# Reordering the passage from the quantised feed-forward layer into relative-position self-attention

## What is computed

```python
x = _layernorm(x + _L0_xattn_ref(x, ctx, ctx, mask, fside, ...))     # 16 heads of 16, additive bias and mask
x = _layernorm(x + _L0_ffn_ref(x, weight, gamma, beta))
x = _layernorm(x + _L1_attn_ref(x, Wq, bq, Wk, bk, Wv, bv, Wo, bo, rel_k, rel_v))

def _L0_ffn_ref(x, weight, gamma, beta):
    xn = (x - mean(x)) * rsqrt(var(x) + 1e-5) * gamma + beta
    scale = max(max(abs(xn)), 1e-8) / 127                # one number over all tokens of all sequences
    xq = round(clip(xn / scale, -127, 127)) * scale
    absw = abs(weight); delta = 0.7 * mean(absw)
    mask = absw > delta
    alpha = sum(absw * mask) / max(sum(mask), 1)
    return xq @ (alpha * sign(weight) * mask).T

def _L1_attn_ref(h, ...):                                 # MAX_REL = 20
    idx = clip(pos[None, :] - pos[:, None], -20, 20) + 20
    attn = softmax((q @ k.T + einsum('bhqd,qkd->bhqk', q, rel_k[idx])) / 4)
    w = attn @ v + einsum('bhqk,qkd->bhqd', attn, rel_v[idx])
    return w @ Wo.T + bo
```

## Time and profile before

| | |
|---|---|
| device time, median of 3 runs | 926.36 us (924.04 to 928.03) |
| the profiled execution | 927.1 us, span 925.3 us, mean granted clock 0.98 |
| busy, share of the span | PE 93%, PEld 67%, DVE 74%, ACT 67%, POOL 45% |
| passage, 275 to 326 us | last round of block one to `peaks(0, 0)` of block two |

### The profile page before, as it was taken

How to read it: one execution, slowest core, us unless ns; L and a number is a source line. 1 busy time by engine, 2 the same in 40 slices (tenths; PEclk the granted TensorE clock), 3 DMA queues, 4 the chain that set the end, 5 groups by cost and what they waited for, 6 DMA issues and landing times. The chain is left out here.

```text
span 925.3 us, 21117 instructions
## 1 busy us (share of the span) xinstructions
PE 861.7 (93%) x7006; PEld 621.4 (67%) x7017; DVE 681.9 (74%) x2515; ACT 620.9 (67%) x1608; POOL 413.0 (45%) x428
## 2 busy tenths in 40 slices
PE   9998989999987788999999999897999999999996
PEld 7876766777666466777777776675666666655554
DVE  4988888888877656687686676525888878866875
ACT  4548677777762367787787787735888888864441
POOL 2256246567342345434444342243455555326432
PEclk9999999999998899999999999997999999999998
DMA  9334100000005187797787788440000000000001
GB/s 327 115 113 117 42 24 24 25 24 13 13 25 204 55 279 241 226 277 219 244 251 227 242 256 253 140 165 4 27 27 28 27 28 24 2 2 1 24 24 46
DMA packets 96960, 101.89 MB, mean 110 GB/s; under 512 B 26877, under 2 KB 92157, under 8 KB 96598
## 3 DMA queue, kind: packets, MB, share of 16 engines
q1 hardware_dynamic: 96292, 100.20, 34.6%
q10 hardware_dynamic: 562, 0.35, 0.1%
HBM read 48.70 MB, written 51.82 MB: 109 GB/s over the span
## 5 line engine op out<-in xcount | busy, mean ns | idle before, releaser
L222 PE MATMUL bank<-x_feat,w_all_mats 128*128 128x256 f32 x384 | 94.6, 391 | 2.1 <-ACT q_full L340 0.6
L2746 POOL TENSOR_TENSOR bnd<-bnd,consts 128x60 f32<-128x60 f32 x64 | 18.1, 303 | 149.5 <-DMA bnd<-band_scratch 149.5
L222 PEld LDWEIGHTS bank<-x_feat,w_all_mats 128*128 128x128 f32 x384 | 71.0, 192 | 15.4 <-ACT rw L2404 4.3
L2364 ACT ACTIVATE bias_area<-bias_area,mq_two 128x256 f32<-128x256 f32 x128 | 66.2, 529 | 0.0
L1680 DVE COPY q_heads<-bank 128x512 f32<-128x512 f32 x64 | 42.7, 686 | 28.8 <-PE bank L1386 28.8
L1427 PE MATMUL bank<-dist,rw 128*128 128x512 bf16 x277 | 62.9, 379 | 0.7 <-issue 0.2
L845 ACT ACTIVATE q_heads<-bank 128x512 f32<-128x512 f32 x64 | 37.7, 589 | 37.9 <-PE bank L664 37.9
L2537 DVE COPY q_heads<-bank 128x512 f32<-128x512 f32 x64 | 41.4, 683 | 26.2 <-PE bank L2036 26.2
L931 DVE COPY q_heads<-bank 128x512 f32<-128x512 f32 x64 | 41.8, 683 | 25.3 <-PE bank L664 25.3
L837 ACT ACTIVATE Sx<-Sx,mq 128x256 f32<-128x256 f32 x128 | 54.4, 499 | 5.7 <-DVE mq L923 5.6
L1672 DVE CUSTOM_DVE_ANT_0 Sx<-bank,bias_area 128x256 f32<-128x256 f32 x128 | 46.5, 419 | 14.3 <-PE bank L1372 13.9
(11 more groups left out here) (275 smaller groups left out, 2494.8 us busy)
## 6 DMA issues: line engine op xcount, KB each, us to landing
dist<-skew_scratch SPq DMA_DIRECT2D x64, 296.0 KB, 4.2
skew_scratch<-rw SPq DMA_DIRECT2D x32, 588.0 KB, 4.5
bnd<-band_scratch SPq DMA_DIRECT2D x64, 108.0 KB, 2.7
band_scratch<-bias_area SPq DMA_DIRECT2D x32, 162.0 KB, 2.7
band_scratch<-bias_area SPq DMA_DIRECT2D x32, 148.0 KB, 2.5
skew_scratch<-dist SPq DMA_DIRECT2D x4, 1024.0 KB, 8.5
context_values<-dist SPq DMA_DIRECT2D x8, 512.0 KB, 2.6
v_two<-context_values SPq DMA_DIRECT2D x8, 512.0 KB, 3.5
```

The source lines that it names most:

```text
L222: last = pe.matmul(dst[:, m * S:(m + 1) * S], w[:, k, m * P:(m + 1) * P], rhs[:, k, :], start=(k == 0), stop=(k == FT - 1))
L2364: last = act.activation(rows_of(n, g)[:, t, :], rows_of(n, g)[:, t, :], ACT.Exp, bias=mq_two[:, n % 2, g, t:t + 1], scale=-1.0, accum_out= ...
```

## The change

Five edits, all in this passage:

- `ternary_mask` is cut in three. The mask and the product stand between `normalise(B - 1, 0)` and `(B - 1, 1)`, the two sums between the halves of `fold_here(B - 2)` (now `fold_begin`, `fold_end`), the signs behind it. PE's matmul of the weight sum goes ahead of `turn_back(B - 1, 0)`.
- The last normalisation of block one is scaled by DVE (`normalise_here`), and POOL keeps the power only.
- In block two PE begins with six 128x128 products of the identity that nothing reads, `turn_whole(0)` and the bias product stand ahead of the first ternary product, and each context product behind a turning. ACT's list follows.
- DVE's three clips stand together, the two memsets are cut in four and stand between the norms of sequences 0 and 1.
- The first two stores to `skew` are cut in halves by pairs of heads, with a semaphore `r_first` for the first half; `load_dist(0)` waits for that alone.

```diff
@@ block one, tensor
                     project_context(pe, 0)
+                    pe.wait_ge(w_sum, 1)
+                    pe.matmul(t_bank[0][:, 0:1], ones_w[:, :], wst[:, 0:1], start=True, stop=True).then_inc(w_mm, 1)
                     pe.wait_ge(y_steps, 4 * (B - 2) + 1)
                     pe.wait_ge(ot_sb, NQ * B)
                     turn_back(B - 1, 0)
                     project_context(pe, 1)
                     pe.wait_ge(normed, TT * (B - 1) + 1)
                     turn_back(B - 1, 1)
-                    pe.wait_ge(w_sum, 1)
-                    pe.matmul(t_bank[0][:, 0:1], ones_w[:, :], wst[:, 0:1], start=True, stop=True).then_inc(w_mm, 1)
                     project_context(pe, 2)
@@ block one, vector
+                    def normalise_here(t):
+                        dve.wait_ge(rstd_ready, t + 1)
+                        for i in range(TT):
+                            last = dve.tensor_scalar(x_tok[:, t, i, :], y_sb[:, i, :], mv[:, i, 0:1],
+                                                     rstd[:, i:i + 1], ALU.subtract, ALU.mult)
+                        last.then_inc(kept, 1)
...
                     normalise(B - 1, 0)
+                    ternary_mask()
                     normalise(B - 1, 1)
                     fold_step = Steps(dve, f_last, 0, 4)
                     fold_statistics(B - 2)
-                    fold_here(B - 2, fold_step)
+                    fold_begin(B - 2, fold_step)
+                    ternary_counts()
+                    fold_end(B - 2, fold_step)
+                    ternary_signs()
                     dve.wait_ge(biased, B)
                     norm_begin(dve, y_steps, B - 1, y_mm, B, m_bank, True, parts=(0, 1, 2))
                     fold_peak_here(B - 2, fold_step)
-                    ternary_mask()
+                    normalise_here(B - 1)
                     fold_statistics(B - 1)
-                    fold_here(B - 1, fold_step)
+                    fold_begin(B - 1, fold_step)
+                    fold_end(B - 1, fold_step)
@@ block one, gpsimd
-                    normalise(B - 1)
+                    pool.wait_ge(y_steps, 4 * B)
+                    pool.tensor_tensor(rstd[:, :], ve[:, :], neghalf[:, :], ALU.pow).then_inc(rstd_ready, 1)
@@ block two, tensor
-                    project_context(pe, KV_EARLY)
+                    for i in range(6):
+                        pe.matmul(m_bank[:, 0:P], ident[:, :], ident[:, :], start=True, stop=True)
                     turn_whole(0)
-                    ternary_product(0)
-                    project_context(pe, KV_EARLY + 1)
-                    turn_whole(1)
-                    ternary_product(1)
-                    turn_normed(0)
                     pe.wait_ge(bv_wide, 1)
                     for m in range(FT):
                         pe.matmul(o_bank[:, 0:D], aT[:, m, 0:P], wo[:, m, :], start=(m == 0), stop=False)
...
+                    ternary_product(0)
+                    project_context(pe, KV_EARLY)
+                    turn_whole(1)
+                    project_context(pe, KV_EARLY + 1)
+                    ternary_product(1)
+                    turn_normed(0)
                     project_q(0)
@@ block two, scalar
                             act.wait_ge(r_out[i - TT], 16 * (b + 1))
+                            if b == 0:
+                                act.wait_ge(r_first, 16 * TT)
...
                     copy_whole(0)
-                    keep_context(act, KV_EARLY)
                     make_whole(1)
-                    keep_context(act, KV_EARLY + 1)
-                    copy_whole(1)
-                    copy_normed(0)
                     act.wait_ge(bias_mm, 1)
                     act.activation(bias_rep[:, :], o_bank[:, 0:D], ACT.Copy).then_inc(bias_sb, 1)
+                    copy_whole(1)
+                    keep_context(act, KV_EARLY)
+                    keep_context(act, KV_EARLY + 1)
+                    copy_normed(0)
@@ block two, vector
                     ff_statistics(0)
-                    clip(2)
-                    round_(2)
+                    for slot in range(4):
+                        dve.wait_ge(v_stored[slot], 16 * 2)
+                    dve.memset(dist_pairs[:, 1, 0:H // 4, 0:P - REL, :], 0.0)
                     ff_normalise(0)
+                    dve.memset(dist_pairs[:, 1, H // 4:, 0:P - REL, :], 0.0)
                     add_ff(1)
                     ff_statistics(1)
+                    dve.wait_ge(q_clip, FF_EARLY)
+                    dve.wait_ge(affine_stored, 16 * (B - FF_EARLY))
+                    dve.memset(dist_pairs[:, 0, 0:H // 4, P + REL:S, :], 0.0)
                     ff_normalise(1)
+                    dve.memset(dist_pairs[:, 0, H // 4:, P + REL:S, :], 0.0)
...
-                    dve.memset(dist_pairs[:, 0, :, P + REL:S, :], 0.0)
-                    dve.memset(dist_pairs[:, 1, :, 0:P - REL, :], 0.0)
@@ block two, sync
+                    def store_first(t, u):
+                        if u == 0:
+                            sp.wait_ge(r_filled, t + 1)
+                        lo = (0, EW - RW)[t]
+                        sp.dma_start(skew[0, t, 2 * u:2 * u + 2, :, lo:lo + RW, :].rearrange("h p e v -> p h (e v)"),
+                                     rw[:, t, 2 * u:2 * u + 2, :, :].rearrange("p h e v -> p h (e v)"))\
+                            .then_inc(r_first if u == 0 else r_out[t], 16)
...
-                    for m in range(FT):
-                        store_rel(0, TT * m)
-                        store_rel(0, TT * m + 1)
-                        load_dist(2 * m)
-                        load_dist(2 * m + 1)
+                    for u in range(2):
+                        for t in range(TT):
+                            store_first(t, u)
+                    load_dist(0)
+                    load_dist(1)
+                    for t in range(TT):
+                        store_rel(0, TT + t)
+                    load_dist(2)
+                    load_dist(3)
```

25 lines of the change are left out of this document (15 added, 10 removed).

## The result

The changed kernel took 917.93 us in the median of 8 runs (915.49 to 919.86), the kernel before 924.15 beside it; the ratio is 0.9923 with a 95% interval of 0.9902 to 0.9944. I had said 923.4 against a median of 926.36, that is -3.0 us or 0.997, with a range down to 920.5. By the medians the gain is 6.2 us, by the means 7.0 (917.9 against 924.9); with the changed kernel's 14 runs and the 91 of the kernel before that ran beside the experiments it is 7.5 by the means.

What follows compares the result with a forecast made beforehand. DVE was taken to bound the end of block one, and scores and transfers together the first peaks. -2.6 + 1.1 - 1.5 = -3.0 us against the median 926.36 gave 923.4 us, range 920.5 to 926.2.

Steps and rivals of the forecast that it cites:

- What bounds the kernel: DVE finishes block one last; at the first peaks the scores on PE and the chain of transfers end together.
- Part A: End of block one: ternary work moved ahead of the residual sum and the last scaling on DVE, -2.6 us.
- Part B: Start of block two to `project_q(0)`: 12.1 us instead of 11.00, +1.1 us, with 3.1 us at the low clock.
- the price of the identity products: Start of block two: six identity products bounded by their weight loads, 12 x 0.205 = 2.5 us at 2.4 GHz.
- my lower bound: Start of block two: identity products take 1.4 us if 128-column loads pace like half of a 256-column product.
- my last rival: Start of block two: clock stays at 1.2 GHz until `project_q(0)`, +6.3 us in all, 932.7 us; chance 0.04.
- Part C: `project_q(0)` to `peaks(0, 0)`: 15.0 us instead of 16.48, -1.5 us, bounds -0.2 and -2.7.
- a sign of being wrong: At the first peaks: `peaks(0, 0)` still released by DMA instead of waiting for the scores.
- Carried to the end unchanged.: Behind the first peaks (326.16) the rounds keep PE fed, so the shift there lasts to the end.
- the rival in which the clock stays up: PE idles only some 3 us between the blocks: -2.7, -0.1 and -2.7, together -5.5 us, 920.9 us; chance 0.24.
- A's bound (-3.4): End of block one: the gain if the residual sum is not late at all, -3.4 us.

Runs made afterwards that it cites:

- e1: The kernel before with the edits of block one alone (ternary weights in pieces, last scaling on VectorE): 921.22 us, ratio 0.9954.
- e11: The kernel before with the last scaling of block one on VectorE alone, ternary weights in their old place: 925.99 us, ratio 1.0005.
- e10: The kernel before with the ternary weights in pieces alone, the last scaling still on GpSimd: 925.24 us, ratio 0.9994.
- e8: The changed kernel with nine more identity products that nothing reads, in PE's waits ahead of the first scores: 920.56 us, ratio 0.9944.
- e2: The kernel before with block two's new lists alone (identity products, PE's and ACT's new order, three clips together): 925.43 us, ratio 0.9983.
- e9: The changed kernel with PE's and ACT's lists, stores and loads as before and no identity products: 917.83 us, ratio 0.9917.
- e4: The changed kernel without the six identity products: 922.27 us, ratio 0.9966.
- e6: The changed kernel with the first two stores whole, as before: 918.29 us, ratio 0.9927.
- e13: The kernel before with the clip and rounding of sequence 3 on VectorE moved behind the copy of the keys: 924.23 us, ratio 0.9984.
- e3: The kernel before with the four memsets in their new places and the halved first stores alone: 927.23 us, ratio 1.0013.
- e7: The changed kernel with the two whole memsets back in their old places: 919.78 us, ratio 0.9943.

## Why the prediction was wrong, point by point

**What bounds the kernel.** Right: DVE ended block one, and two chains, scores and transfers, ended together at the first peaks. e1 shows the transfers as a bound of their own, with the clock up: 16.2 us behind Q, where the scores end at 13.2.

**Part A was mis-sized: -2.6 predicted, -3.44 measured.** Behind `ve` it went as computed (1.57 us against 1.59). The residual sum is late by 0.45 us instead of 0.86 (12.00 us after the last sum, against 11.55), in part because the ternary product takes 0.69 us instead of 0.93 where POOL's scaling doesn't run beside it (0.69 in e11 too). And from the last statistics to block two it is 7.16 us instead of 7.61, of which I had said "as before". Of these 0.45, 0.36 lie on DVE, between the statistics and the first reduction for the global peak:

```profile
292.32 0.18 DVE L980 BATCH_NORM_AGGREGATE ffn_mv<-ffn_st 128x2 f32<-128x6 f32 x1 [0.22 <-issue]
...
295.41 0.16 DVE L1016 TENSOR_REDUCE pmax<-amax 128x1 f32<-128x8 f32 x1
```
```profile
289.63 0.25 DVE L980 BATCH_NORM_AGGREGATE ffn_mv<-ffn_st 128x2 f32<-128x6 f32 x2
...
292.75 0.16 DVE L1027 TENSOR_REDUCE pmax<-amax 128x1 f32<-128x8 f32 x1
```

The first pair is before (4.34 us from the statistics), the second the changed kernel (3.98). It is 4.34 with the scaling on POOL in e10 too and 3.99 with the scaling on DVE in e11, so the gap goes with the scaling's place; why is not shown. The remaining 0.1 lies in the two small products on PE for the peak. The two errors of part A are 0.4 and 0.45.

**Part B was mis-sized: +1.1 predicted, -0.2 measured.** The step that failed is the price of the identity products. I took their weight loads as the bound, 2.5 us at the full clock. They took 2.0 from start to start, and 1.2 us of that at the low clock. The fillers of e8 take 0.39 us for two instructions and 0.83 for six, a pace of 0.11 to 0.14 us, so 12 cost about 1.4 at the full clock by this estimate, my lower bound. That is 1.1 of the 1.3 us by which part B was off. The low clock inside it was nearly as forecast, 3.4 us for 3.1. The row I had leaned on the earlier trace rows was a pair of loads at the end of a busy stretch with nothing behind it, and the time of a pair is not a pace. That the list itself brings nothing was right (e1, e2, e9); that the clock would decide here was right too, but it takes e4's version of the list for it to do harm, where 3 us are lost by the mechanism of my last rival, a third of its price.

**Part C was mis-sized: -1.5 predicted, -2.5 and -1.8 in the two profiles.** Both chains ended where I had put them: scores 13.2 us behind Q at the full clock (13.21 measured), transfers 13.8 (14.00, 13.57 and 13.48). I had expected 1.8 of the 3.1 us that low clock had cost to remain; the first profile had none, the second about 1.3. So in the first profile the transfers held the peaks (2.63 us of waiting for DMA), which I had named as a sign of being wrong, and in the second the scores did. That the transfers end where I said is in part luck: the cause of the long fill was wrong, the halves bring 0.85 us and not 1.6 (e6), and I counted from 16.5 where the old transfers by themselves end at 16.2 (e1).

**"Carried to the end unchanged."** Nearly right in the profiles (at the first peaks the changed kernel's two executions are 6.1 and 5.4 us ahead, at turning 4 5.9 and 6.4); what is missing to the 7 to 7.5 of the means I put down to the clock, which is an estimate and not shown by an experiment. Over the 91 runs of the kernel before, those with a mean clock of 0.989 or 0.990 took 923.3 us (13 runs), those at 0.981 to 0.983 took 927.7 (17). The changed kernel's mean clock is higher by 0.0035 over its 14 runs, which at that rate is 1.9 us. By that estimate about 5.6 us are work and waits taken away, and 1.9 go with the clock; it does not say whether the clock is cause or company. I had no term for the second, and my base, one profiled execution with 13.6 us of low clock in the passage, was one draw of a wide spread: e2 and e13, with the same block one, have 6.8 us there and none behind Q, e3 has 20.4. And it held a long low stretch that a start of block two 3 us earlier no longer has: there the seven other kernels with the whole of block one's edits and work for PE at once have 3.4 us like the changed one, e4 with its long wait has 10.2, e10 has 10.2 as well, and before, e2, e3, e11 and e13 have 6.8.

**The range.** It ended 2.6 us above the result. Its lower end was set by the rival in which the clock stays up, with A at 2.7. Had A's bound (-3.4) been carried into that rival, as I had worked it out in the text, the range would have reached 920.2; with the lower bound of the identity products 919.1; the last 1.2 I leave to the clock outside the passage, by the estimate above.

**In a sentence.** Of the 7.5 us by the means, block one is worth 4.7 (2.9 of it at turning 4 in its profile), the moved memsets with the clips together about 2 to 3, the halved stores nothing that shows, and the new lists nothing that shows, since their identity products pay back what the order costs.

## What to carry to other kernels

Two edits that each remove a cover from the other's bound must be costed together: alone they moved the start of block two by 1.5 and -0.2 us, together by 3.4, the largest gain here. A moved instruction should be read with what is queued behind it, as the wait of another engine may be due to that one. And where a product of real work can open a stretch on TensorE after idle time, as in the old list, it did here what the filler products of the new list do, and for nothing (e9).

## What the runs showed of the hardware

A clip (a TENSOR_SCALAR of one input) queued behind a memset on VectorE kept GpSimd's copy waiting through the memset: 2.42 us (e7) and 2.66 (before) instead of 0.90, and 0.90 with the same memset and the instruction elsewhere (e13). A VectorE product with two inputs took 0.93 us beside GpSimd's scaling (before, e2) and 0.69 without (the changed kernel, e11). Executions of one kernel differ in where the granted clock falls, and in the kernel before the mean clock of a run goes with its time, 923.3 us at about 0.990 against 927.7 at about 0.982.
